# A fused attention and feed-forward kernel: the output projection in split float32r, and the last head group's projection moved into the next row

## The chip, the core and the metric

The kernel runs on one core of a Trainium2 chip. The metric is the device time of one execution in microseconds (us).

## The reference

For each of 8 rows of 512 tokens by 256 channels: layer norm without weights, then the sum of the input, an attention branch and a feed-forward branch, both fed from the normalised input.

```python
q, k = rope(xn @ Wq), rope(xn @ Wk)        # 32 query heads, 8 key heads, 64 each
v = xn @ Wv                                # 4 query heads share a key head
scores = where((j <= i) & (i - j < 128), q k^T / 8, -inf)
attn_out = (softmax(scores) @ v) @ Wo      # Wo: 2048 x 256
h = fwht(xn * SU_ug) / 64
h = silu(h @ Wgate.T * s_gate) * (h @ Wup.T * s_up)          # 1024 wide
ffn_out = (fwht(h * SU_dp) / 64) @ Wdown.T * s_down
out = x + attn_out + ffn_out
```

## The kernel before, in words

All in float32. The Hadamard transforms are folded into the weights in a prologue. Products with Wq, Wk, Wv and the gate and up weights are made from float32r operands: every operand is held as a high part (a copy rounded to float32r) and a low part (the difference), and `three` (L701) accumulates high x high, high x low and low x high. Scores, transposes, the product with V, the down projection and the output projection use plain float32; each such matmul shows as two records in the trace (a transpose as one).

After the prologue there are 8 rows (`b`). A row is:
- The feed-forward part: for j of 0 to 7 a gate and an up product (`hidden`), ScalarE's silu, VectorE's multiply, and `down(j)`. Query rope products of head groups 1 to 3 lie between them. At its end VectorE adds the result to `acc`.
- The attention part: 32 steps (8 key heads `g` by 4 blocks `i` of 128 tokens), done in 35 slots, n = 0 to LAST_SLOT. TensorE's slot n (loop at L879) issues `scores(n)`, `transposes(n-2)`, the slot's fillers, and `values_mixed(n-3)` (the product O with V). A step with i = 0 sees one block of keys, all others see two; so S of a slot with n mod 4 = 0 and O of one with n mod 4 = 3 are half as large.

`fillers(b, n)` (L81) is the hand-written order of the remaining TensorE work: V products, rope products by the table ROPE_SLOTS (L72), transposes of the next row's x (slot 25), and output projections ("wo"). An output projection `project_out(g, part)` (L854) multiplies two blocks of 128 tokens of head group g by two 128-row tiles of Wo: 4 matmuls of 256 columns, 16 such calls a row. VectorE's `wo_add` (L634) adds the result to `acc`. Before the change, the calls lie in slots 6, 7, 10, 11, ..., 30, 31, 34, and the last one after slot 34. The rope fillers are in slots 3, 4, 8, 9, 12, 13, 16, 17, 20, 21, 28, 29, and the next row's first query products in 32 and 33.

The chain of one step n across engines:
- VectorE `fold(n)` (L645): masks within S (L650) and takes the negative maximum (L652).
- ScalarE `exps(n)` (L475), which needs the maximum. `scores(n+2)` waits for it.
- VectorE `normalise(n)` (L655, in slot n+1): reciprocal and multiply.
- TensorE transposes into TR (slot n+2); ScalarE copies (L485); GpSimd masks into p_cur and p_prev (L396, L400).
- TensorE O (L849, slot n+3). It waits for the masks and, since O is one PSUM bank, for the copy of the O before it.
- ScalarE `o_copy(n)` (L487) copies O to `o_t`, as its last work of the slot; `project_out` waits for these copies by `o_copied`.

VectorE's order in a slot is fold(n), normalise(n-1), then the adds and rope multiplies of the slot's fillers. Projections, rope products, V, gate and up all take turns in the two banks of PROJ; `USES` (L99) is the list of the turns, and a user of a bank waits until the turn two before it has been read.

SP's queue issues the DMAs: for every head group, copies of rotated q and k into stacked tiles; at a row's end the output DMA, which waits for all of the row's `wo_add` (L338), and behind it the next row's stacks and the load of x. GpSimd's first work in a row is the rotation of q group 0, then it waits for the output DMA (L408) and copies x into `acc`, then come rotations 1 to 3.

In the prologue VectorE makes low parts of the weights, the rope multiplies of the first heads, and at last eight scalings of the down weights into `wd_sb` (L622). TensorE waits for them (L780) and for the DMA of Wo (L781) before row 0.

## Time and profile before

| | us |
|---|---|
| median of 3 runs | 1518.5 (1518.24 to 1518.95) |
| profiled execution | 1521.65 |
| its span, first to last instruction | 1519.8 |
| TensorE matmul busy | 1464.1 |
| VectorE busy | 1002.0 |
| ScalarE busy | 729.1 |
| GpSimd busy | 593.9 |
| mean granted TensorE clock | 0.993 |

The span is one profiled execution; the other 1.85 us of it lie around the first and last instruction. Matmuls are pipelined and their ends are modelled: the distance between starts is the pace, the duration is not. L-numbers are lines of the kernel before. In a timeline the columns are start, duration, engine, line, operation, output<-input, count, and in brackets the idle time before it with what ended it.

### The profile page before, as it was taken

The page shows a single profiled execution, that of the slowest core. Times are in us where ns is not written, and L with a number is a line of the kernel's source. Part 1 is how long each engine was busy: PE and PEld are TensorE (multiplying, and loading weights), DVE is VectorE, ACT ScalarE, POOL GpSimd, SP SyncE. Part 2 cuts the span into 40 slices and gives each one's busy share as a digit, 9 for nine tenths or more (in the row PEclk, how much of TensorE's full clock was granted, in tenths as well). Part 3 has the DMA queues.
Part 4 walks back from the last instruction along what each step waited for, and adds up shares of the span by engine and source line. Part 5 has one row for each costly group of instructions (what it writes and reads, how often), then busy time and mean ns, then how long its engine had stood idle before and what let it go on. Part 6 is the DMA issues. An engine that isn't in the chain of part 4 may idle for free. (4 is left out here: it accounts for less than half of the span.)

```text
span 1519.8 us, 25035 instructions
## 1 busy us (share of the span) xinstructions
PE 1464.1 (96%) x8424; PEld 1023.8 (67%) x8424; DVE 1002.0 (66%) x1702; ACT 729.1 (48%) x2738; POOL 593.9 (39%) x629
## 2 busy tenths in 40 slices
PE   5599999999999999999999999999999999999998
PEld 3476667766677666766668666676667766677665
DVE  5537884488835887358863788537884488835785
ACT  1226562365614656146642566326562365614655
POOL 3214543155422554125542354314543155421553
PEclk9799999999999999999999999999999999999999
DMA  7101211022020120202202111101212022020120
GB/s 285 35 21 42 51 35 53 18 56 50 22 70 20 44 51 13 69 22 56 50 19 52 43 43 43 47 23 43 55 31 57 16 58 46 22 56 21 43 54 25
DMA packets 51087, 70.67 MB, mean 46 GB/s; under 512 B 13072, under 2 KB 24848, under 8 KB 50448
## 3 DMA queue, kind: packets, MB, share of 16 engines
q1 hardware_dynamic: 49968, 68.34, 18.0%
q8 instruction: 69, 1.13, 0.3%
q10 hardware_dynamic: 992, 0.73, 0.2%
q14 instruction: 58, 0.48, 0.1%
HBM read 14.49 MB, written 4.19 MB: 12 GB/s over the span
## 5 line engine op out<-in xcount | busy, mean ns | idle before, releaser
L475 ACT ACTIVATE e_sb<-S,negmax 128x128 f32<-128x128 f32 x1024 | 361.9, 368 | 93.3 <-DVE negmax L652 93.3
L396 POOL TENSOR_SCALAR_AFFINE_SELECT p_cur<-pt_sb 128x512 f32<-128x512 f32 x256 | 185.1, 723 | 541.6 <-ACT pt_sb L485 493.0
L485 ACT ACTIVATE pt_sb<-TR 128x512 f32<-128x512 f32 x256 | 153.2, 598 | 235.8 <-PE TR L832 207.2
L823 PE MATMUL S<-k_stack,q_stack 64*128 64x256 f32 (+1 forms) x2048 | 264.5, 377 | 0.0
L861 PE MATMUL PROJ<-wo_sb,o_t 128*128 128x256 f32 x1024 | 244.2, 381 | 5.6 <-ACT o_t L490 4.6
L823 PEld LDWEIGHTS S<-k_stack,q_stack 64*128 64x128 f32 x2048 | 166.4, 187 | 106.8 <-issue 80.3
L661 DVE TENSOR_TENSOR e_sb<-e_sb,rinv 128x512 f32<-128x512 f32 x256 | 223.3, 872 | 8.7
L650 DVE COPY_PREDICATED S<-later_key,S 128x512 f32<-128x512 int8 x192 | 133.4, 695 | 132.0 <-PE S L823 132.0
L475 ACT ACTIVATION_READ_ACCUMULATOR e_sb<-S,negmax 128x1 f32 x1024 | 211.6, 207 | 0.0
L861 PEld LDWEIGHTS PROJ<-wo_sb,o_t 128*128 128x128 f32 x1024 | 184.7, 190 | 33.2 <-issue 12.6
L368 POOL TENSOR_TENSOR qy<-prod 128x512 f32<-128x512 f32 x64 | 81.6, 1275 | 291.1 <-DVE prod L573 265.9
L572 DVE TENSOR_TENSOR prod<-PROJ,cos_sb 128x512 f32<-128x512 f32 x160 | 109.4, 684 | 129.2 <-PE PROJ L705 129.2
L400 POOL TENSOR_SCALAR_AFFINE_SELECT p_prev<-pt_sb 128x512 f32<-128x512 f32 x192 | 191.8, 999 | 0.0
L652 DVE TENSOR_REDUCE negmax<-S 128x4 f32<-128x512 f32 x256 | 176.9, 691 | 8.8
L470 ACT ACTIVATE pt_sb<-PROJ 128x512 f32<-128x512 f32 x64 | 38.3, 598 | 298.8 <-PE PROJ L705 298.8
L849 PE MATMUL O<-p_cur,v_sb 128*64 128x256 f32 x1024 | 167.6, 405 | 7.2 <-POOL p_cur L396 5.4
L832 PE MATMUL TR<-ident,e_sb 128*128 128x128 f32 x1024 | 167.7, 286 | 4.8 <-DVE e_sb L661 3.1
L832 PEld LDWEIGHTS TR<-ident,e_sb 128*128 128x128 f32 x1024 | 107.2, 140 | 79.5 <-issue 57.9
L703 PE MATMUL PROJ<-xt_hi,wq_hi 128*128 128x512 f32 x256 | 116.1, 453 | 15.7 <-DVE wq_lo L530 14.5
L490 ACT ACTIVATE o_t<-O 128x256 f32<-128x256 f32 x256 | 100.1, 391 | 50.0 <-PE O L849 49.9
L632 DVE TENSOR_TENSOR p_cur<-PROJ,pt_sb 128x512 f32<-128x512 f32 x64 | 44.3, 691 | 117.4 <-PE PROJ L705 117.4
L803 PE MATMUL S<-wd_sb,p_cur 128*128 128x256 f32 x512 | 119.6, 379 | 0.0
(79 smaller groups left out, 2011.8 us busy)
## 6 DMA issues: line engine op xcount, KB each, us to landing
q_stack<-qy SPq DMA_DIRECT2D x512, 64.0 KB, 2.0
k_stack<-ky SPq DMA_DIRECT2D x256, 64.0 KB, 2.0
x_in<-x SPq DMA_DIRECT2D x8, 512.0 KB, 4.0
out<-acc SPq DMA_DIRECT2D x8, 512.0 KB, 3.1
gu_stage<-w_gate_up SPq DMA_DIRECT2D x2, 1024.0 KB, 6.5
wq_stage<-wq SPq DMA_DIRECT2D x2, 1024.0 KB, 10.1
wo_sb<-wo SPq DMA_DIRECT2D x1, 2048.0 KB, 11.0
down_stage<-w_down SPq DMA_DIRECT2D x1, 1024.0 KB, 8.5
```

The source lines that it names most:

```text
L396: nc.gpsimd.affine_select(out=p_cur[:, n % 2, :, :], in_=pt_sb[:, :, :], compare_op=ALU.is_ge, fill=0.0, base=0, pattern=[[0, REP], [1, P] ...
L400: nc.gpsimd.affine_select(out=p_prev[:, n % 2, :, :], in_=pt_sb[:, :, :], compare_op=ALU.is_gt, fill=0.0, base=0, pattern=[[0, REP], [-1, P]],
L475: last = nc.scalar.activation(e_sb[:, n % 2, r, :], s_heads(n, 1)[:, r, :], ACT.Exp, bias=negmax[:, n % 2, r:r + 1], accum_out=rowsum[:, n ...
L485: nc.scalar.activation(pt_sb[:, :, :], TR[:, :, :], ACT.Copy).then_inc(t_copied, 1)
L650: nc.vector.copy_predicated(own, later_key[:, :, :], earlier).then_inc(s_folded, 1)
L652: nc.vector.tensor_reduce(negmax[:, n % 2, :], own, axis=AX.X, op=ALU.max, negate=True).then_inc(max_done, 1)
L661: nc.vector.tensor_tensor(e, e, r, ALU.mult).then_inc(norm_done, 1)
L803: last = nc.tensor.matmul(S4[:, t, 0:C], h_sb[j % 2][:, t * P:(t + 1) * P], wd_sb[:, j, :], start=j == 0, stop=j == FT - 1)
L823: last = nc.tensor.matmul(dst, q_stack[rows, g % 2, slot, i * P:(i + 1) * P], k_stack[rows, g % 2, k0:k1], start=True, stop=True)
L832: last = nc.tensor.transpose(TR[:, r, :], e_sb[:, n % 2, r, :], ident[:, :])
L849: last = nc.tensor.matmul(O[odd * D:(odd + 1) * D, 0:2 * P].rearrange("p (m q) -> p m q", m=2), v_sb[:, i - earlier, g * D:(g + 1) * D], p ...
L861: last = nc.tensor.matmul(dst[:, t * C:(t + 1) * C], o_t[:, m, tok:tok + P], wo_sb[:, 2 * g + m, :], start=m == 0, stop=m == 1)
```

## The change

What it does:
- Wo and the attention output are held as high and low parts in float32r, and `project_out` uses `three`: 12 matmuls of 256 columns for 4.
- VectorE makes the low part of O: `o_low(n-4)` in slot n, directly behind `fold(n)`, from slot 4 on, counted by a new semaphore `o_split`. `values_mixed` and `project_out` wait for `o_split` instead of `o_copied`.
- The slots are shifted by one: projections in slots 7, 8, 11, 12, ..., 31, 32; rope parts in 9 and 10, 13 and 14, and so on; the next row's first query products in 33 and 34. Slots 5, 6 and 26 have no filler, as slots 5 and 24 had none.
- The last head group's two projections and their adds are done in the next row's feed-forward part, behind the first and second gate and up products; those of the last row at the end. So the row's output DMA waits for them there.
- In the prologue ScalarE makes the high part of Wo and VectorE the low part (4096 columns each), VectorE's ahead of the `wd_sb` scalings. TensorE waits for it before row 0. Staging tiles are laid out differently.

```diff
-    ROPE_SLOTS = {("q", 4, 0): (3, 4), ("k", 1, 0): (8, 9), ("q", 5, 0): (12, 13),
-                  ("q", 6, 0): (16, 17), ("q", 7, 0): (20, 21), ("k", 0, NEXT): (28, 29)}
+    ROPE_SLOTS = {("q", 4, 0): (3, 4), ("k", 1, 0): (9, 10), ("q", 5, 0): (13, 14),
+                  ("q", 6, 0): (17, 18), ("q", 7, 0): (21, 22), ("k", 0, NEXT): (29, 30)}
...
-        if n in (STEPS, STEPS + 1) and b + 1 < BATCH:
-            found.append(("q", b + 1, 0, n - STEPS))
-        if n >= TT + 2 and n % TT >= 2:
+        if n in (STEPS + 1, STEPS + 2) and b + 1 < BATCH:
+            found.append(("q", b + 1, 0, n - STEPS - 1))
+        if n >= TT + 3 and (n + 1) % TT < 2:
-            found.append(("wo", b, n // TT - 1, n % TT - 2))
+            found.append(("wo", b, (n + 1) // TT - 2, (n + 1) % TT))
...
+                if b and not n:
+                    USES.append(("wo", b - 1, NKV - 1, j))
...
# scalar, prologue
+            act.wait_ge(wo_in, 16)
+            nc.scalar.activation(wo_p[0][:, :, :], wo_stage[:, :, :], ACT.Copy).then_inc(w_hi, 1)
# scalar, o_copy
-                    nc.scalar.activation(o_t[:, :, i * P:(i + 1) * P],
+                    nc.scalar.activation(o_p[0][:, :, i * P:(i + 1) * P],
# vector
+            def o_low(row, n):
+                i = n % TT
+                dve.wait_ge(o_copied, row * STEPS + n + 1)
+                low(o_p[1][:, :, i * P:(i + 1) * P], O[:, 0:2 * P].rearrange("p (m q) -> p m q", m=2),
+                    o_p[0][:, :, i * P:(i + 1) * P]).then_inc(o_split, 1)
...
             products(0, "q", 0, 1)
+            dve.wait_ge(w_hi, CT + 2)
+            low(wo_p[1][:, :, :], wo_stage[:, :, :], wo_p[0][:, :, :]).then_inc(w_lo, 1)
...
-                hidden(0)
-                hidden(1)
+                for j in HIDDEN_AFTER[0]:
+                    hidden(j)
+                    if b:
+                        if not j:
+                            o_low(b - 1, STEPS - 1)
+                        wo_add(b - 1, NKV - 1, j)
...
                     if n < STEPS:
                         fold(n)
+                    if 4 <= n:
+                        o_low(b, n - 4)
                     if 1 <= n <= STEPS:
                         normalise(n - 1)
...
-                wo_add(NKV - 1, 1)
+            o_low(BATCH - 1, STEPS - 1)
+            for part in range(2):
+                wo_add(BATCH - 1, NKV - 1, part)
# tensor
+            def project_out(row, g, part):
+                dst = bank("wo", row, g, part)
+                pe.wait_ge(o_split, row * STEPS + TT * g + 2 * part + 2)
+                for t in range(2):
+                    for m in range(2):
+                        tok = (2 * part + t) * P
+                        last = three(dst[:, t * C:(t + 1) * C], [a[:, m, tok:tok + P] for a in o_p],
+                                     [a[:, 2 * g + m, :] for a in wo_p], m == 0, m == 1)
+                last.then_inc(proj_ready, 1)
...
-            pe.wait_ge(wo_in, 16)
+            pe.wait_ge(w_lo, CT + 2)
...
                     if n >= 1:
-                        pe.wait_ge(o_copied, b * STEPS + n)
+                        pe.wait_ge(o_split, b * STEPS + n)
...
                             hidden(name, j)
+                        if b and not n:
+                            project_out(b - 1, NKV - 1, j)
                         if j:
                             down(j - 1)
...
-                project_out(NKV - 1, 1)
+            for part in range(2):
+                project_out(BATCH - 1, NKV - 1, part)
```

## Rows read from the trace of the kernel before

**Rows 1.** The page's first part: busy us, share of the span, instructions.
```profile
PE 1464.1 (96%) x8424; PEld 1023.8 (67%) x8424; DVE 1002.0 (66%) x1702; ACT 729.1 (48%) x2738; POOL 593.9 (39%) x629
```

**Rows 2.** Stretches: length, busy of PE, PEld, DVE, ACT, POOL, granted clock; one feed-forward part.
```profile
429.20:476.40 47.20, 47.05 (x204) 37.90 (x202) 17.03 (x31) 9.04 (x13) 8.58 (x7) 1.00 0.21 56
```

**Rows 3.** Timelines of TensorE and of VectorE, slots 12 and 13 of row 3.
```profile
702.74 0.71 PE L823 MATMUL S<-k_stack,q_stack 64*128 64x128 f32 x8
...
705.37 0.65 PE L849 MATMUL O<-p_cur,v_sb 128*64 128x256 f32 x4
...
706.39 1.13 PE L823 MATMUL S<-k_stack,q_stack 64*128 64x256 f32 x8
...
709.44 0.65 PE L849 MATMUL O<-p_cur,v_sb 128*64 128x256 f32 x4
...
710.45 0.49 PE L823 MATMUL S<-k_stack,q_stack 64*128 64x256 f32 x2
...
703.62 0.75 DVE L650 COPY_PREDICATED_SCALAR S<-later_key,masked 128x512 f32 x1 [0.56 <-PE S L823]
...
707.68 0.70 DVE L650 COPY_PREDICATED S<-later_key,S 128x512 f32<-128x512 int8 x1 [0.48 <-PE S L823]
708.41 0.69 DVE L652 TENSOR_REDUCE negmax<-S 128x4 f32<-128x512 f32 x1
709.02 0.17 DVE L657 RECIPROCAL rinv<-rowsum 128x4 f32<-128x4 f32 x1
```

**Rows 4.** Timeline of TensorE: an output projection, and two float32r matmuls of a rope product.
```profile
700.34 1.89 PE L861 MATMUL PROJ<-wo_sb,o_t 128*128 128x256 f32 x8
...
704.12 0.41 PE L704 MATMUL PROJ<-xt_lo,wq_hi 128*128 128x512 f32 x1
...
705.06 0.39 PE L705 MATMUL PROJ<-xt_hi,wq_lo 128*128 128x512 f32 x1
```

**Rows 5.** Groups by line and form, VectorE adds from PSUM: busy us, mean ns.
```profile
L642 DVE TENSOR_TENSOR acc<-PROJ,acc 128x512 f32<-128x512 f32 x128 | 87.1, 680 | 40.6 <-PE PROJ L861 40.6
...
L676 DVE TENSOR_TENSOR acc<-S,acc 128x1024 f32<-128x1024 f32 x8 | 9.8, 1225 | 21.5 <-PE S L803 21.5
```

**Rows 6.** Timelines: a rotation; slots 8, 24, 28 of row 1; 24 and 31 of row 7.
```profile
312.87 1.26 POOL L368 TENSOR_TENSOR qy<-prod 128x512 f32<-128x512 f32 x1 [2.65 <-PE O L849]
...
322.41 0.71 PE L823 MATMUL S<-k_stack,q_stack 64*128 64x128 f32 x8
...
386.73 0.71 PE L823 MATMUL S<-k_stack,q_stack 64*128 64x128 f32 x8
...
389.92 1.68 DVE L556 TENSOR_SCALAR prod<-x_in,moments,rstd 128x256 f32<-128x256 f32 x4
...
401.73 0.72 PE L823 MATMUL S<-k_stack,q_stack 64*128 64x128 f32 x8
...
1479.40 0.71 PE L823 MATMUL S<-k_stack,q_stack 64*128 64x128 f32 x8
...
1502.80 1.14 PE L823 MATMUL S<-k_stack,q_stack 64*128 64x256 f32 x8
```

**Rows 7.** Timeline from slot 31 of row 1 into the feed-forward part of row 2.
```profile
413.83 1.14 PE L823 MATMUL S<-k_stack,q_stack 64*128 64x256 f32 x8
...
419.51 0.37 ACT L490 ACTIVATE o_t<-O 128x256 f32<-128x256 f32 x1
...
420.02 0.65 PE L849 MATMUL O<-p_cur,v_sb 128*64 128x256 f32 x4 [0.15 <-ACT o_t L490]
...
427.62 1.97 PE L861 MATMUL PROJ<-wo_sb,o_t 128*128 128x256 f32 x8 [0.57 <-ACT o_t L490]
429.24 0.59 PE L703 MATMUL PROJ<-xt_hi,wgu_hi 128*128 128x512 f32 x1
```

**Rows 8.** The prologue: timeline of VectorE, and a stretch (0.57 is the clock).
```profile
59.67 3.43 DVE L622 SCALAR_TENSOR_TENSOR wd_sb<-S,su_mid_sb,o_t 128x256 f32<-128x256 f32 x8
...
40.00:60.00 20.00, 7.06 (x16) 5.02 (x17) 14.29 (x14) 6.77 (x6) 4.65 (x3) 0.57 0.06 14
```

More of the change, by code:

```diff
@@ L109, in attention_and_ffn_block @@
             USES += fillers(b, n)
-        USES.append(("wo", b, NKV - 1, 1))
+    USES += [("wo", BATCH - 1, NKV - 1, part) for part in range(2)]
     TURN = {what: u for u, what in enumerate(USES)}
@@ L134, in sem @@
             return ctx.enter_context(nc.semaphore(name))
-        wq_p = [sb(f"wq_{s}", [P, CT, NH * D], f32r) for s in ("hi", "lo")]
-        wk_p = [sb(f"wk_{s}", [P, CT, NKV * D], f32r) for s in ("hi", "lo")]
-        wv_p = [sb(f"wv_{s}", [P, CT, NKV * D], f32r) for s in ("hi", "lo")]
+        with ExitStack() as prologue:
+            wq_stage = prologue.enter_context(nc.sbuf_tensor("wq_stage", [P, CT, NH * D], fp32))
+            wo_stage = prologue.enter_context(nc.sbuf_tensor("wo_stage", [P, NH * D // P, C], fp32))
+            kv_stage = prologue.enter_context(nc.sbuf_tensor("kv_stage", [P, 2, CT, NKV * D], fp32))
+        wq_lo = sb("wq_lo", [P, CT, NH * D], f32r)
+        wo_lo = sb("wo_lo", [P, NH * D // P, C], f32r)
+        wk_lo = sb("wk_lo", [P, CT, NKV * D], f32r)
+        wv_lo = sb("wv_lo", [P, CT, NKV * D], f32r)
+        wq_p = [sb("wq_hi", [P, CT, NH * D], f32r), wq_lo]
+        wo_p = [sb("wo_hi", [P, NH * D // P, C], f32r), wo_lo]
+        wk_p = [sb("wk_hi", [P, CT, NKV * D], f32r), wk_lo]
+        wv_p = [sb("wv_hi", [P, CT, NKV * D], f32r), wv_lo]
         wgu_p = [sb(f"wgu_{s}", [P, CT, 2 * F], f32r) for s in ("hi", "lo")]
         wd_sb = sb("wd_sb", [P, FT, C])
-        wo_sb = sb("wo_sb", [P, NH * D // P, C])
         cos_sb = sb("cos_sb", [P, T])
@@ L164, in attention_and_ffn_block @@
         with ExitStack() as prologue:
-            wq_stage = prologue.enter_context(nc.sbuf_tensor("wq_stage", [P, CT, NH * D], fp32))
             gu_stage = prologue.enter_context(nc.sbuf_tensor("gu_stage", [P, CT, 2 * F], fp32))
@@ L171, in attention_and_ffn_block @@
         k_stack = sb("k_stack", [P, 2, T])
-        staging_rest = sb("staging_rest", [P, 5120])
+        o_lo = sb("o_lo", [P, REP // 2, T], f32r)
         ky = sb("ky", [P, 2, T])
@@ L181, in attention_and_ffn_block @@
         p_prev = sb("p_prev", [P, 2, REP, P])
-        o_t = sb("o_t", [P, REP // 2, T])
+        scale_d_b = sb("scale_d_b", [P, C])
+        had = sb("had", [P, 2, P])
+        o_p = [sb("o_hi", [P, REP // 2, T], f32r), o_lo]
         xn = prod[:, 0:2, :].rearrange("p a (t c) -> p (a t) c", c=C)
@@ L574, in products, with wo_add @@
                                         ).then_inc(prod_done, 1)
+            def o_low(row, n):
[3 more added lines that the diff above has]
+                    o_p[0][:, :, i * P:(i + 1) * P]).then_inc(o_split, 1)
+            def wo_add(row, g, part):
+                bank, filled = place("wo", row, g, part)
+                k = 2 * g + part
+                dve.wait_ge(proj_ready, filled)
+                if k >= 2:
+                    dve.wait_ge(wo_added, (row + 1) * 2 * NKV + k - 1)
+                a = acc[:, 2 * part:2 * part + 2, :]
+                nc.vector.tensor_tensor(a, PROJ[:, bank, :].rearrange("p (t c) -> p t c", t=2), a, ALU.add
+                                        ).then_inc(wo_added, 1)
             row_stats(0)
@@ L632, in hidden @@
                     nc.vector.tensor_tensor(h_sb[j % 2], PROJ[:, bank, :], silu_sb, ALU.mult).then_inc(h_done, 1)
-                def wo_add(g, part):
-                    bank, filled = place("wo", b, g, part)
-                    k = 2 * g + part
-                    dve.wait_ge(proj_ready, filled)
-                    if k >= 2:
-                        dve.wait_ge(wo_added, (b + 1) * 2 * NKV + k - 1)
-                    a = acc[:, 2 * part:2 * part + 2, :]
-                    nc.vector.tensor_tensor(a, PROJ[:, bank, :].rearrange("p (t c) -> p t c", t=2), a, ALU.add
-                                            ).then_inc(wo_added, 1)
                 def fold(n):
@@ L691, in _ @@
                         if kind == "wo":
-                            wo_add(m, part)
+                            wo_add(row, m, part)
                         elif kind == "x":
@@ L852, in values_mixed @@
                     last.then_inc(pv_done, 1)
-                def project_out(g, part):
-                    dst = bank("wo", b, g, part)
-                    pe.wait_ge(o_copied, b * STEPS + TT * g + 2 * part + 2)
-                    for t in range(2):
-                        for m in range(2):
-                            tok = (2 * part + t) * P
-                            last = nc.tensor.matmul(dst[:, t * C:(t + 1) * C], o_t[:, m, tok:tok + P],
-                                                    wo_sb[:, 2 * g + m, :], start=m == 0, stop=m == 1)
-                    last.then_inc(proj_ready, 1)
                 for n in range(4):
@@ L885, in _ @@
                         if kind == "wo":
-                            project_out(m, part)
+                            project_out(row, m, part)
                         elif kind == "x":
```

28 lines of the change are left out of this document (11 added, 17 removed).

## The prediction

> **What bounds the kernel now.** I read the page first: TensorE is busy 96% of the span, VectorE 66%, ScalarE and GpSimd under half [rows 1]. That says TensorE, but a matmul's recorded end is modelled, so the pace has to be read from starts. The stretch table of a feed-forward part shows TensorE without gaps [rows 2]. Then I read slots of the attention part, from one scores group to the next [rows 3]. A slot is S, transposes, a filler, O. The slots at 702.74 and 706.39 last 3.65 and 4.06 us, and no row of TensorE in them has an idle stretch ahead of it; the longer one has scores of two key blocks. Slots come in periods of four, two with a rope filler and two with an output projection: slots 8 to 23 of that row last 386.73-322.41 = 64.32 us [rows 6], 16.08 a period, and it is TensorE's own work.
>
> The second thing to see in [rows 3] is how close VectorE runs behind. The fold of step n starts 0.88 us after S where S has one block (703.62) and 1.29 us where it has two (707.68). Ahead of them it idled 0.56 and 0.48 us only. From the fold to the end of the reduce is 1.42 us (707.68 to 709.10), while O starts 2.63 and 3.05 us after S.
>
> **Part 1, the projection itself.** One call was 8 records of 256 columns in 1.89 us, the last lasting 0.38: (1.89-0.38)/7 = 0.216 us each, 1.73 in all [rows 4]. It becomes 12 float32r matmuls of 256 columns. The trace has float32r at 512 columns only: four steps from 704.12 to 705.06, 0.235 us each [rows 4]. From below: one pass of 256 columns is half of 0.216, 0.108 us. From above: the cost belongs to the instruction and not to its columns, 0.235. The 512-column row exceeds 0.216 by 0.019; if that excess is fixed, 256 columns take 0.127. I take this, since two fp32 passes of 256 and one float32r pass of 512 agree so nearly that the rate per column is the same. A call is then 1.52 us, 0.21 less; 128 calls save 27 us of TensorE. The ends give 1.30 and 2.82 us.
>
> The weight loads matter here: twelve loads of 128 columns against eight, and half as many columns streamed behind each. The trace shows loads of full 128-row weights keeping up with fp32 matmuls 0.216 apart [rows 4]. The Trainium skill's "TensorE: Matmul & The Clock Gate", in Part 3 on packing small matmuls, says a weight load overlaps a running matmul only where the row group differs. By that rule load and matmul would add up and the projection would lose by the change; in this trace the row group is the same and the pace is still that of the streaming alone, so the rule does not hold for it as stated.
>
> **Part 2, o_low and the wait on it.** VectorE gets one more instruction per step, 256 in all: O (256 columns, PSUM) minus the high part. A PSUM add of 512 columns is 0.68 us and one of 1024 is 1.225 [rows 5]; the slope gives 0.41 us at 256. Behind another instruction it occupies about 0.34, as neighbours overlap by 0.08. Its place is behind the fold: fold, o_low(n-4), normalise(n-1). And O of step n-3 now waits for that o_low instead of for ScalarE's copy. Behind the waiting O on TensorE are the next scores, thus the next fold and everything else.
>
> So a slot has a floor that it did not have. Where S has two blocks: fold at 1.29, reduce 0.73 later, o_low 0.61 after that (708.41 to 709.02), its end 0.41 on: 3.04 us after S. From the release to the start of O is 0.14 (copy end 419.88, O 420.02) [rows 7]. O starts at 3.18, and the next S 1.01 later (709.44 to 710.45): a floor of 4.19, or 3.76 where O has one block. With one block of scores (a fold of 0.75 where the other is 0.70) it is 0.88+0.79+0.61+0.41+0.14 = 2.83, and 3.84 in all. The new order puts the projections in slots with n mod 4 of 3 and 0, the rope parts in 1 and 2. TensorE alone would need 4.06 in a rope slot and 4.06+1.52-6 x 0.235-0.43 = 3.74 in one with a projection and one block of S or O. The floor is at or above each: 3.84+4.19+4.19+3.76 = 15.98 against 16.08 now. Of the 0.43 that the two projections save, 0.33 is given to the wait. Four periods (slots 8 to 23) in eight rows: 32 x -0.10 = **-3.2 us**. VectorE's load is no bound there: o_low takes 0.34 of the 0.5 us it idled.
>
> **Part 3, slots without a filler.** These were short, since O had nothing to wait for. In slots 4 to 7 the mask waits for a rotation that starts at 312.87, held by a DMA, so slot 6 was already stalled. Following it through with the floor, O of slot 5 starts 1.7 us later, O of slot 6 0.6 later, and the scores of slot 8 come at 322.4 as before [rows 6]: **0**. But one projection fewer lies in the stalled stretch, and is paid elsewhere (below).
> Slots 24 to 27 were 401.73-386.73 = 15.0 us [rows 6]. Now: 3.84; then slot 25, whose fold comes 0.6 late behind four normalisations (1.68 in all) and the projection's add, 4.79; slot 26 without a filler 4.19; slot 27 3.76. Sum 16.58, 1.58 more, **+11.0** in seven rows. Slots 28 to 30: 3.84+4.19+4.19 = 12.22 against 12.12, **+0.7**.
> The last row has no work of a next row, so slots 25, 26, 29 and 30 are empty: slots 24 to 30 were 1502.80-1479.40 = 23.40 [rows 6], now 15.98+12.22 = 28.20: **+4.8**.
>
> **Part 4, the row's end.** From the scores of slot 31 (413.83) to the feed-forward part (429.24) is 15.4 us; it holds three projections, and a stall of 0.57 ahead of the last [rows 7], which goes. Now slot 31 takes 3.76. In slot 32 o_low(28) waits for a copy that lies behind a table load and ends at 419.88, 6.04 after slot 31's scores; O starts at 6.65 instead of 5.9, and the next transposes at 7.67. The rest is 5.6: 13.3. Two projections follow in the feed-forward part, where nothing hides them (TensorE had no gap [rows 2]): 3.04. Together 16.3, +0.93 a row, **+6.5** in seven. The output DMA now starts some 9 us later, and behind it in SP's queue stand the next row's stack copies and its x load, in GpSimd's the copy into acc and rotation 1. The rotation needs products that come 15 us into the feed-forward part, the scores need the stacks 47 us in: cost 0. Without that slack it would be the delay itself.
> In the last row o_copy, o_low and O alternate for three steps with nothing beside them, and two projections follow: **+1.1**.
>
> **Part 5, the prologue.** wo needs a high part (ScalarE, idle then: 0) and a low part of 4096 columns, which stands on VectorE ahead of the eight scalings of wd at 59.67, and TensorE waits for both [rows 8]. At the slope of [rows 5] it is 4.5 us: from below. It reads two SBUF tiles while GpSimd rotates; if it were held up as long as those run, 2.5 us more: from above. I take 4.5: the nearest row, the scalings at 59.67, ran beside that rotation at 0.43 each, not held up. The Trainium skill's "SBUF — State Buffer", section on the two sides, says whichever of the two starts first has the shared ports for its whole instruction; by it 4.5 if VectorE wins the race and 2.5 more if GpSimd does; no row shows which. TensorE then idles 5.5 us and not 1. From 40 to 60 us, with TensorE busy 7 of 20, the mean granted clock was 0.57 [rows 8], so mostly the lower of the two levels (1.2 and 2.4 GHz): it had fallen while TensorE idled and rose only after it had resumed. An estimate: half rate for the first 4 us of row 0 costs 2 (0 to 3). **+6.5**.
>
> **Sum**: -3.2+11.0+0.7+4.8+6.5+1.1+6.5 = +27.4 us. The profiled execution took 1521.65 (span 1519.8), so 1549.05; the median of the runs is 1518.5, 3.15 less, so 1545.9: forecast **1546**.
>
> **Rivals.**
> B, it gets faster: O never waits for o_low, TensorE's own work is the sum. For it: 96% busy. The point that decides is whether o_low has ended by 2.9 to 3.1 us after S. Then -27, a row's last stall gone (8 x -0.6 = -5), one projection out of the stalled slots (8 x 1.5 = +12), prologue +6.5: -13.5, **1505**. Against it: [rows 3] put the fold's end at 2.7 alone. 0.13.
> C, a float32r matmul of 256 columns costs as much as one of 512 (0.235), since it is bound by something other than its columns, the weight load say. A call is 2.82 us. In slots with a projection TensorE then exceeds the floor by 1.2: 14 x 8 x 1.2 = 134, and 16 in the feed-forward parts cost 1.3 more, 21: **1700**. The rule in the skill's TensorE page is this rival's mechanism, with load and matmul in series. 0.07.
> D, the floor holds only where there is no filler, because o_low ends some 0.1 us sooner than I put it: the periods get 15.65, so -0.33 x 32, and slots 28 to 30 -0.25 x 8: **1533**. 0.13.
> E, as forecast, and TensorE's longer idling in slots 4 to 7 lowers its clock in each row as it did in the prologue [rows 8]. 3.4 us at half rate is 1.7 a row, 14 in all: **1560**. 0.07.
> My forecast: 0.60.
>
> **Range.** The pace of 0.108 takes 3 off, one of 0.14 adds 13; the latencies (0.05 per slot, 230 slots) are worth 12 either way; the prologue -2 to +4. With D and E inside: 1524 to 1572. B and C are left out, 0.20. A measurement of this kernel can tell about 0.2%, 3 us. Faster: B, and little of D: 0.14. Same: 0.03. Slower: 0.83.
>
> **What the changed profile would show.** Starts of the projection's matmuls 0.127 us apart; o_low at 0.41; ahead of O an idle stretch put down to VectorE's o_lo, near 0.1 us in filled slots and 1.5 in empty ones; slots of 4.19; the first gate matmul at about 68 us. I am wrong if O starts as soon as its filler ends (B), if the projection's starts are over 0.2 apart (C), or if slots 25 and 26 together stay under 8 us.

## The result, and the profile after

The changed kernel takes **1547.8 us** (median of 4 runs, 1546.6 to 1547.8) where the kernel before takes 1518.4 (4 runs, 1517.1 to 1519.0): ratio 1.0193, 95% interval 1.0175 to 1.0211. The forecast was 1546. The profiled execution has a span of 1546.1 us, 26.3 more than before; the mean granted clock is 0.992.

The page's first part, then three groups by line and form (busy us, mean ns, idle time before with its releasers):

```profile
PE 1429.3 (92%) x8936; PEld 1041.7 (67%) x8936; DVE 1095.0 (71%) x1959; ACT 744.3 (48%) x2739; POOL 544.0 (35%) x629
```

```profile
L885 PE MATMUL O<-p_cur,v_sb 128*64 128x256 f32 x1024 | 167.2, 398 | 70.3 <-DVE o_lo L538 42.1 <-POOL p_cur L406 14.7
...
L730 PE MATMUL PROJ<-wo_hi,o_lo 128*128 128x256 f32 x512 | 143.6, 281 | 0.0
...
L538 DVE TENSOR_TENSOR o_lo<-O,o_hi 128x256 fp32r<-128x256 f32 x256 | 106.5, 416 | 16.2 <-ACT o_hi L501 15.6
```

Against [rows 1], TensorE is busy 35 us less and the span is 26 us longer. The wait is new: 42.1 us of TensorE's idle time end with o_lo, all of it ahead of O. The transposes wait 2.7 us for VectorE's normalisation. The idle time is not the loss. 23.5 of the 42.1 us lie in slots 5 and 6. Slot 6 was stalled before the change too (it took 5.28 us in row 1), and slots 0 to 7 are no longer than they were (the table below). On the other side, part of the time that the projections save went into slots whose projection now ends earlier and whose O does not.

TensorE and VectorE in slots 8 and 9 of row 3 (one block of scores with a projection, then two blocks with a rope part; [rows 3] has slots 12 and 13):

```profile
697.62 0.74 DVE L667 COPY_PREDICATED_SCALAR S<-later_key,masked 128x512 f32 x1
697.66 0.36 PE L728 MATMUL PROJ<-wo_hi,o_hi 128*128 128x256 f32 x1
...
698.09 0.28 PE L728 MATMUL PROJ<-wo_hi,o_hi 128*128 128x256 f32 x1
...
698.80 0.28 PE L728 MATMUL PROJ<-wo_hi,o_hi 128*128 128x256 f32 x1
...
699.00 0.41 DVE L538 TENSOR_TENSOR o_lo<-O,o_hi 128x256 fp32r<-128x256 f32 x1
699.03 0.28 PE L730 MATMUL PROJ<-wo_hi,o_lo 128*128 128x256 f32 x1
...
699.56 0.65 PE L885 MATMUL O<-p_cur,v_sb 128*64 128x256 f32 x4 [0.25 <-DVE o_lo L538]
...
700.58 1.14 PE L859 MATMUL S<-k_stack,q_stack 64*128 64x256 f32 x8
701.87 0.70 DVE L667 COPY_PREDICATED S<-later_key,S 128x512 f32<-128x512 int8 x1 [0.82 <-PE S L859]
702.60 0.69 DVE L669 TENSOR_REDUCE negmax<-S 128x4 f32<-128x512 f32 x1
703.21 0.41 DVE L538 TENSOR_TENSOR o_lo<-O,o_hi 128x256 fp32r<-128x256 f32 x1
...
703.77 0.65 PE L885 MATMUL O<-p_cur,v_sb 128*64 128x256 f32 x4
...
704.79 1.14 PE L859 MATMUL S<-k_stack,q_stack 64*128 64x256 f32 x8
```

From 698.09 to 698.80 are six steps from one matmul of 256 columns to the next, 0.118 us each. The last projection matmul starts at 699.03, o_lo ends at 699.41, O starts at 699.56: 0.15 later. In the next slot the same chain, fold 1.29 after S, reduce, o_lo, O 0.15 after that, makes 704.79-700.58 = 4.21 us.

With no filler the wait is bare. TensorE in slots 5 and 6 of row 1, and these two slots as stretches (length, busy of PE, PEld, DVE, ACT, POOL, clock, DMA):

```profile
318.09 0.65 PE L885 MATMUL O<-p_cur,v_sb 128*64 128x256 f32 x4 [1.47 <-DVE o_lo L538]
...
322.30 0.65 PE L885 MATMUL O<-p_cur,v_sb 128*64 128x256 f32 x4 [1.47 <-DVE o_lo L538]
```

```profile
314.90:319.11 4.21, 2.74 (x23) 1.68 (x21) 4.05 (x8) 2.49 (x11) 1.23 (x1) 1.00 0.27 62
319.11:323.31 4.20, 2.73 (x22) 1.68 (x20) 3.08 (x6) 1.65 (x8) 3.36 (x5) 1.00 0.00 0
```

The prologue, where [rows 8] stood, and the first stretch of row 0:

```profile
58.03 4.42 DVE L538 TENSOR_TENSOR wo_lo<-wo_stage,wo_hi 128x4096 fp32r<-128x4096 f32 x1
58.19 5.38 POOL L378 TENSOR_TENSOR qy<-prod 128x512 f32<-128x512 f32 x1 [14.88 <-DVE prod L584]
62.36 3.22 DVE L650 SCALAR_TENSOR_TENSOR wd_sb<-S,su_mid_sb,scale_d_b 128x256 f32<-128x256 f32 x8
...
65.68 0.76 PE L728 MATMUL PROJ<-xt_hi,wgu_hi 128*128 128x512 f32 x1 [5.46 <-DVE wd_sb L650]
```

```profile
65.60:77.40 11.80, 11.72 (x43) 9.54 (x44) 2.18 (x4) 1.20 (x2) 0.17 (x1) 0.82 0.34 90
```

The span up to the start of the last matmul, cut at the starts of S and of the first gate product of each row. Times are in us, summed over the rows named; where a mean is given, its difference is the sum over the seven rows.

| stretch | before | after | difference |
|---|---|---|---|
| up to the first gate matmul | 63.20 | 65.68 | +2.5 |
| feed-forward of row 0 | 47.14 | 48.99 | +1.9 |
| feed-forward, rows 1 to 7, mean | 47.24 | 49.95 | +19.0 |
| slots 0 to 7, 8 rows | 226.1 | 223.1 | -3.0 |
| slots 8 to 23, 8 rows | 514.6 | 514.9 | +0.3 |
| slots 24 to 27, rows 0 to 6 | 105.0 | 116.9 | +11.9 |
| slots 28 to 30, rows 0 to 6 | 84.9 | 86.6 | +1.7 |
| slot 31 to the feed-forward part, rows 0 to 6 | 107.8 | 93.0 | -14.8 |
| last row, slots 24 to 30 | 23.40 | 28.42 | +5.0 |
| last row, slot 31 to the last matmul | 12.50 | 14.38 | +1.9 |

They sum to +26.4, the difference of the spans but for rounding. In slots 8 to 23 nothing is left of what the projection saves: a call takes 1.73-1.42 = 0.31 us less of TensorE, the 64 calls there 20 us, and the stretch is as long as before.

### The profile page after: what moved, and what is told of

Same layout as the page of the kernel before. It is cut to its first block, busy times and chain, and to the rows that moved or that the text cites. A ratio compares the mean times of both kernels' runs of the same rounds, so it can differ in the third digit from the quotient of the medians.

```text
span 1546.1 us, 26317 instructions
## 1 busy us (share of the span) xinstructions
PE 1429.3 (92%) x8936; PEld 1041.7 (67%) x8936; DVE 1095.0 (71%) x1959; ACT 744.3 (48%) x2739; POOL 544.0 (35%) x629
## 3 DMA queue, kind: packets, MB, share of 16 engines
HBM read 14.49 MB, written 4.19 MB: 12 GB/s over the span
## 4 chain that ended last, share of the span: by engine, by line
PE 64%; DVE 21%; ACT 5%; issue 5%; POOL 4%; DMA 0%; POOLq 0%; ACTq 0%; DVEq 0%
PE S L859 13%; PE O L885 13%; PE PROJ L728 9%; PE PROJ L730 8%; PE PROJ L729 8%; PE S L839 7%; PE TR L868 5%; DVE S L667 5%; DVE negmax L669 5%; POOL p_cur L406 4%; ACT pt_sb L496 3%; DVE o_lo L538 2%; DVE prod L583 2%; DVE e_sb L678 2%; DVE prod L584 2%
## 5 line engine op out<-in xcount | busy, mean ns | idle before, releaser
L678 DVE TENSOR_TENSOR e_sb<-e_sb,rinv 128x512 f32<-128x512 f32 x256 | 229.1, 895 | 8.7
L885 PE MATMUL O<-p_cur,v_sb 128*64 128x256 f32 x1024 | 167.2, 398 | 70.3 <-DVE o_lo L538 42.1
L378 POOL TENSOR_TENSOR qy<-prod 128x512 f32<-128x512 f32 x64 | 85.8, 1341 | 301.6 <-DVE prod L584 274.2
L728 PE MATMUL PROJ<-wo_hi,o_hi 128*128 128x256 f32 x512 | 152.7, 298 | 0.0
L885 PEld LDWEIGHTS O<-p_cur,v_sb 128*64 128x64 f32 x1024 | 57.4, 135 | 140.5 <-POOL p_cur L406 70.9
L730 PE MATMUL PROJ<-wo_hi,o_lo 128*128 128x256 f32 x512 | 143.6, 281 | 0.0
L729 PE MATMUL PROJ<-wo_lo,o_hi 128*128 128x256 f32 x512 | 143.2, 280 | 0.0
L410 POOL TENSOR_SCALAR_AFFINE_SELECT p_prev<-pt_sb 128x512 f32<-128x512 f32 x192 | 134.1, 698 | 0.0
```

Of the source, the lines that this page charges most:

```text
L678: nc.vector.tensor_tensor(e, e, r, ALU.mult).then_inc(norm_done, 1)
L728: nc.tensor.matmul(dst, lhs[0], rhs[0], start=first, stop=False)
L729: nc.tensor.matmul(dst, lhs[0], rhs[1], start=False, stop=False)
L730: return nc.tensor.matmul(dst, lhs[1], rhs[0], start=False, stop=last)
L885: last = nc.tensor.matmul(O[odd * D:(odd + 1) * D, 0:2 * P].rearrange("p (m q) -> p m q", m=2), v_sb[:, i - earlier, g * D:(g + 1) * D], p ...
```

## The experiments

The theory is the prediction's: O waits for o_low behind the fold, which sets a floor for each slot. Rivals after the result: VectorE is simply too full for 256 more instructions; the new order itself is what costs; float32r at 256 columns gains too little. Ratios are against the kernel before, run beside each of them: median 1518.1 for experiments 3, 10 and 11, and 1518.7 or 1518.8 for the others.

**1. o_low ahead of the fold.** The same instructions, in another order.

```diff
+                    if 4 <= n:
+                        o_low(b, n - 4)
                     if n < STEPS:
                         fold(n)
-                    if 4 <= n:
-                        o_low(b, n - 4)
```

> The changed kernel with one edit: VectorE does o_low(n-4) ahead of fold(n) and not behind it. The work of every engine is the same. Theory A (O waits for an o_low that stands behind the fold, which sets a floor of 4.2, 3.85 or 3.77 us per slot): o_low is done by about 1.4 us after the scores, before O wants to start even in a slot without filler, so slots fall to TensorE's own work. Periods of four: 3.67+4.06+4.06+3.67 = 15.5 instead of 16.07, four of them in 8 rows -18; slots 24 to 27 about 15.2 instead of 16.67 in seven rows, -10; slots 28 to 30 -0.5 each row, -4; the last row's slots 24 to 30 about 21.8 instead of 28.4, -6; slots 5 to 7 stay bound by the rotation. About 1508 us, faster than both kernels. Rival (VectorE's added load itself holds TensorE up): the load is unchanged, so 1540 or more.

Measured: **1513.1** us, ratio 0.9956 (0.9940 to 0.9972): 34.7 us come back, and this version is a little faster than the kernel before. TensorE and VectorE in slot 9 of row 3:

```profile
689.68 1.14 PE L859 MATMUL S<-k_stack,q_stack 64*128 64x256 f32 x8
690.32 0.42 DVE L538 TENSOR_TENSOR o_lo<-O,o_hi 128x256 fp32r<-128x256 f32 x1 [0.42 <-ACT o_hi L501]
...
690.98 0.70 DVE L667 COPY_PREDICATED S<-later_key,S 128x512 f32<-128x512 int8 x1 [0.24 <-PE S L859]
...
692.75 0.65 PE L885 MATMUL O<-p_cur,v_sb 128*64 128x256 f32 x4
...
693.76 1.14 PE L859 MATMUL S<-k_stack,q_stack 64*128 64x256 f32 x8
```

o_lo stands in time in which VectorE waited for S anyway, its copy having ended: the fold still starts 1.30 us after S, as in [rows 3]. O starts with no idle time ahead of it, and the slot is 4.08. Slots 8 to 23 take 61.8 us a row instead of 64.4. The expectation said 1508, though its own four terms add up to -38 and so to 1510. Those stretches gave -36 between the traces (-20.8, -9.8, -1.6 in seven rows, -4.2), and slots 0 to 7 gave +1.1 instead of nothing. The clock is in that +1.1: its falls cost these slots some 11 us in this execution. Slots 5 and 6 of two rows (columns as above; the windows of the first row are cut at 862.00, and its slot 6 ends at 861.41):

```profile
853.90:856.80 2.90, 2.75 (x22) 1.68 (x20) 2.87 (x6) 1.48 (x6) 0.18 (x1) 1.00 0.40 90
856.80:862.00 5.20, 3.59 (x25) 2.01 (x25) 4.09 (x8) 2.95 (x14) 4.36 (x5) 0.93 0.01 3
862.00:866.60 4.60, 4.60 (x30) 3.34 (x26) 3.08 (x6) 3.12 (x16) 1.49 (x3) 0.71 0.19 43
...
1034.40:1037.30 2.90, 2.75 (x22) 1.68 (x20) 2.87 (x6) 1.48 (x6) 0.12 (x1) 1.00 0.40 90
1037.30:1042.00 4.70, 3.04 (x24) 1.57 (x22) 4.15 (x8) 2.39 (x11) 4.00 (x4) 1.00 0.02 3
```

In the first row the granted clock falls behind the stall of slot 6, in the second it does not. Slots 0 to 7 take 28.2 to 28.7 us in the rows where it falls and 26.6 where it does not. It falls in six rows of this execution. The runs scatter from 1506 to 1516, the shorter ones with the higher mean clock (0.985 to 0.991).

**2. o_low cut loose from O.** It subtracts the high part from itself, so that the low part of the attention output is zero, and O waits for the copy alone.

```diff
-                low(o_p[1][:, :, i * P:(i + 1) * P], O[:, 0:2 * P].rearrange("p (m q) -> p m q", m=2),
+                low(o_p[1][:, :, i * P:(i + 1) * P], o_p[0][:, :, i * P:(i + 1) * P].bitcast(fp32),
...
-                        pe.wait_ge(o_split, b * STEPS + n)
+                        pe.wait_ge(o_copied, b * STEPS + n)
```

> The changed kernel with o_low in its place behind the fold, 256 of them, but reading only the high part in SBUF (so the low part of the attention output is zero: that part of the product is left out), and O waiting for ScalarE's copy alone, as before the change. Theory A: the load without the wait costs nearly nothing, 1500 to 1510 us. Rival (VectorE's load): still 1540 or more. Both its inputs are in SBUF, so it may be held up at times where GpSimd works, which could add some us.

Measured: **1533.2** us, ratio 1.0099 (1.0079 to 1.0120), a miss. The wait of O is gone, and another stands in its place, together with a longer o_lo. Two groups of this kernel:

```profile
L868 PE MATMUL TR<-ident,e_sb 128*128 128x128 f32 x1024 | 167.7, 286 | 46.0 <-DVE e_sb L678 44.0 <-ACT pt_sb L496 1.6
...
L538 DVE TENSOR_TENSOR o_lo<-o_hi 128x256 fp32r<-128x256 f32 x256 | 147.7, 577 | 11.6 <-ACT o_hi L501 11.0
```

The transposes now wait 44 us for the normalisation, and o_lo takes 577 ns where it took 416. VectorE and GpSimd of row 3:

```profile
700.91 0.63 POOL L406 TENSOR_SCALAR_AFFINE_SELECT p_cur<-pt_sb 128x512 f32<-128x512 f32 x1 [2.65 <-ACT pt_sb L496]
701.03 0.79 DVE L538 TENSOR_TENSOR o_lo<-o_hi 128x256 fp32r<-128x256 f32 x1
...
704.97 0.63 POOL L406 TENSOR_SCALAR_AFFINE_SELECT p_cur<-pt_sb 128x512 f32<-128x512 f32 x1 [2.66 <-ACT pt_sb L496]
705.29 0.59 DVE L538 TENSOR_TENSOR o_lo<-o_hi 128x256 fp32r<-128x256 f32 x1
```

Both times o_lo ends 0.28 us after GpSimd's mask (701.54 and 701.82, 705.60 and 705.88), whenever it began. The experiment had a side effect of its own: by reading SBUF in place of PSUM, o_lo became an instruction that waits for GpSimd.

**3. The same with one SBUF input.** o_low multiplies the high part by zero; the low part of the attention output is zero.

```diff
+                nc.vector.tensor_scalar(o_p[1][:, :, i * P:(i + 1) * P],
+                    o_p[0][:, :, i * P:(i + 1) * P].bitcast(fp32), 0.0, None, ALU.mult).then_inc(o_split, 1)
...
+                        pe.wait_ge(o_copied, b * STEPS + n)
```

> As the kernel with o_low cut loose from O (1533.2), but o_low reads one SBUF tile instead of two: a multiplication of the high part by zero (the low part of the attention output is zero in both). It must still end before nobody's O; only normalise stands behind it. Theory P: the 1533 came from two SBUF inputs that share something with GpSimd (o_low took 577 ns on average, 1432 at most). Then o_low now takes under 350 ns each time, normalise goes back to about 895 ns, slots 12, 16 and 20 to 3.66, and the total is about 1506 (range 1502 to 1512). Theory L: VectorE has simply no room for one more instruction ahead of normalise, whatever it reads. Then the transposes still wait for normalise and it stays above 1522.

Measured: **1525.6** us, ratio 1.0049 (1.0032 to 1.0066). The time is on the side of theory L (over 1522), and the transposes wait 34.6 us for the normalisation; but the condition for telling P from L, an o_lo under 0.35 us each time, was not met, since the mean is 0.526. The 39 o_lo with no GpSimd instruction beside them take 0.28 to 0.30 us; the longest are 1.42:

```profile
901.78 1.27 POOL L380 TENSOR_TENSOR qy<-prod 128x512 f32<-128x512 f32 x1
901.79 1.42 DVE L590 TENSOR_SCALAR o_lo<-o_hi 128x256 fp32r<-128x256 f32 x1
...
903.33 0.92 DVE L678 TENSOR_TENSOR e_sb<-e_sb,rinv 128x512 f32<-128x512 f32 x1
...
904.30 0.66 PE L868 MATMUL TR<-ident,e_sb 128*128 128x128 f32 x4 [0.80 <-DVE e_sb L678]
```

So the contention does not need two SBUF inputs, and theory P named its cause too narrowly. Held-up o_lo and late normalisation lie on one path, and these two kernels do not say how much VectorE's plain load would cost alone. They cannot be read as the price of a kernel whose O never waits; experiments 1 and 5 can.

**4. The projection back in fp32.** 4 fp32 matmuls of the high parts; the low parts are made and waited for, and not used.

```diff
-                        last = three(dst[:, t * C:(t + 1) * C], [a[:, m, tok:tok + P] for a in o_p],
-                                     [a[:, 2 * g + m, :] for a in wo_p], m == 0, m == 1)
+                        last = nc.tensor.matmul(dst[:, t * C:(t + 1) * C], o_p[0][:, m, tok:tok + P].bitcast(fp32),
+                                                wo_p[0][:, 2 * g + m, :].bitcast(fp32), start=m == 0, stop=m == 1)
```

> The changed kernel with the output projection as 4 plain float32 matmuls of the high parts (the low parts are left out of the product), everything else, o_low and its wait too, in place. Theory A: in slots the projection takes 0.31 us more (1.73 against 12 x 0.118), but 0.1 to 0.2 of it lies under the floor: TensorE's own slot is 3.96 against floors of 3.77 and 3.85, so 14 x 0.15 a row, and 2 x 0.33 in the feed-forward part: 8 x 2.8 = +22, about 1570 us. Rival (TensorE is the bound and every us of it counts): 128 x 0.31 = +40, 1588 us.

Measured: **1565.0** us, ratio 1.0309 (1.0294 to 1.0324). It is 5 us under theory A's number and 23 under the rival's. Float32r is worth 17 us in the changed kernel. At 0.31 us a call, 128 calls are 40 us; the rest is hidden under the floor (slots 8 to 23 grow by 8.7 us for 20 us of TensorE).

**5. No low part of O.** The projection multiplies the high part twice, so that the term with the low part of O is not the reference's; there is no o_low, and O and the projection wait for the copy. All matmuls stay.

```diff
-                    if 4 <= n:
-                        o_low(b, n - 4)
...
-                        last = three(dst[:, t * C:(t + 1) * C], [a[:, m, tok:tok + P] for a in o_p],
+                        last = three(dst[:, t * C:(t + 1) * C], [o_p[0][:, m, tok:tok + P]] * 2,
...
-                        pe.wait_ge(o_split, b * STEPS + n)
+                        pe.wait_ge(o_copied, b * STEPS + n)
```

> The changed kernel without o_low: the third matmul of each product uses the high part of the attention output again (12 matmuls and 12 loads as before; the low part is left out), O and the projection wait for ScalarE's copy. Theory A: as low_first and a little lower at the row's end, where O no longer waits for the copy behind the table load plus o_low (-0.4 a row): about 1503 us. Against the changed kernel it gives the price of o_low and its wait together, about 45 us. Rival B of the prediction, which put the kernel at 1505 without the wait, is tested by it too.

Measured: **1501.3** us, ratio 0.9891 (0.9876 to 0.9906), as expected. One group of it:

```profile
L880 PE MATMUL O<-p_cur,v_sb 128*64 128x256 f32 x1024 | 167.4, 405 | 19.8 <-POOL p_cur L406 15.9 <-ACT o_hi L501 3.9
```

o_low with its wait costs 46 us. Experiment 1 keeps the instruction and gives back 35 of them, so the instruction costs some 12 where it stands ahead of the fold, and its place behind the fold the rest. Rival B's sum of 1505 for a kernel whose O never waits is near this 1501; only its condition is not met by the change.

**6. The order alone.** Both edits above, with the fp32 projection and with no low part of Wo either: the new slots and the moved projections of the last head group are all that is left of the change (besides the names of tiles).

```diff
-                    if 4 <= n:
-                        o_low(b, n - 4)
...
+                        last = nc.tensor.matmul(dst[:, t * C:(t + 1) * C], o_p[0][:, m, tok:tok + P].bitcast(fp32),
...
-            low(wo_p[1][:, :, :], wo_stage[:, :, :], wo_p[0][:, :, :]).then_inc(w_lo, 1)
```

> The order alone: slots shifted by one and the last group's projections in the next row's feed-forward part, but the projection as 4 plain float32 matmuls (of the operands' high parts), no o_low, no low part of Wo, and O waiting for ScalarE's copy. Theory A (the order costs: one projection of 1.73 us leaves slots 6 and 7, where TensorE waits for the rotation anyway, +14 in 8 rows; the stall of 0.6 at the row's end goes, -5; with longer idling in slot 5 and 6 the clock falls once a row, 1.7 each as in the run without o_low, +12 or less): 1535 us. Rival (the order is what helps, since it takes a stall away and hides the projections in the feed-forward part): 1510 to 1515 us.

Measured: **1535.7** us, ratio 1.0113 (1.0098 to 1.0128). The new order costs 17 us by itself (14 between the two traces, since the one of the kernel before lies 3 above its median): the feed-forward parts take 3.36 longer, a row's end 2.37 less (seven rows: +7), and slots 0 to 7, with a projection fewer in them and the clock falling, +8 in all. With 4, 5 and the changed kernel it makes a square: fp32 without low parts 1535.7, float32r without 1501.3, fp32 with 1565.0, float32r with 1547.8. The square has a flaw: 1535.7 alone has no low part of Wo, and with it goes 7.0 us up to the end of row 0's feed-forward part (108.8 against 115.8 in experiment 5). So float32r is worth 34 us with that price in it and about 41 without, where O does not wait, which is what 128 calls at 0.31 give, and 17 where it does. In all rows of experiment 6 the clock falls once around slot 6, and slots 0 to 7 take 28.8 to 29.8 us.

**7. The old order, with o_low ahead of the fold.** Old slots and old row end, float32r, low parts; o_low as in experiment 1.

```diff
-    ROPE_SLOTS = {("q", 4, 0): (3, 4), ("k", 1, 0): (9, 10), ("q", 5, 0): (13, 14),
-                  ("q", 6, 0): (17, 18), ("q", 7, 0): (21, 22), ("k", 0, NEXT): (29, 30)}
+    ROPE_SLOTS = {("q", 4, 0): (3, 4), ("k", 1, 0): (8, 9), ("q", 5, 0): (12, 13),
+                  ("q", 6, 0): (16, 17), ("q", 7, 0): (20, 21), ("k", 0, NEXT): (28, 29)}
...
-        if n >= TT + 3 and (n + 1) % TT < 2:
+        if n >= TT + 2 and n % TT >= 2:
-            found.append(("wo", b, (n + 1) // TT - 2, (n + 1) % TT))
+            found.append(("wo", b, n // TT - 1, n % TT - 2))
```

> float32r projection and o_low, o_low(n-4) ahead of fold(n) as in low_first (1513 us), but with the slots and the row's end of the kernel before. Theory A: projections return to slots 6 and 7, where TensorE waits (8 x 1.4 = -11), the clock no longer falls in each row (up to -12), the row's end has its stall back and o_low in it (+0.6 to +1 a row, +7): about 1497 us. Rival (the shift was needed for o_low, the second projection of a group now waits for an o_low of the same slot): over 1513 us.

Measured: **1515.2** us, ratio 0.9977 (0.9968 to 0.9987), a miss by 18. Slots 0 to 7 gained only 2.2 us in all on experiment 1: the clock does not fall here, which was to bring up to 12, but the projection that is back in them was not free, as the expectation had it. And a wait that it priced at the row's end only stands in other slots too: the second projection of a group waits for an o_low of its own slot, 17.8 us in 25 places (7.2 at the rows' ends, 4.9 in slot 27, 4.2 in slot 7). Against the kernel before, the row's end grows from 15.40 to 15.96 and slots 24 to 27 from 14.99 to 15.77, the prologue and row 0 cost 5.4 more, and slots 8 to 23 gain 2.0 a row where the projections save 2.5.

**8. The old order, with o_low behind the fold.**

> As order_back, but o_low behind the fold, as the change has it: float32r and o_low without the change of order. Theory A: the second projection of each group needs an o_low that ends 3.04 us after the slot's scores, and starts at 3.18 instead of 1.5; with 1.42 for itself and 0.68 up to the next scores that slot lasts 5.3 instead of 3.8, seven times a row: +84, less about 11 for a projection back in the stalled slots, so about 1600 us. It shows what the shift by one slot was good for. Rival (VectorE's load or TensorE's work is the bound, the places don't matter): 1550 us or less.

Its edit is that of 7 without the move of o_low. Measured: **1621.1** us, ratio 1.0676 (1.0660 to 1.0692), some 20 above the expectation. VectorE and TensorE, a slot with n mod 4 = 3:

```profile
719.74 1.13 PE L851 MATMUL S<-k_stack,q_stack 64*128 64x256 f32 x8
...
722.38 0.42 DVE L535 TENSOR_TENSOR o_lo<-O,o_hi 128x256 fp32r<-128x256 f32 x1
...
722.94 0.35 PE L720 MATMUL PROJ<-wo_hi,o_hi 128*128 128x256 f32 x1 [1.47 <-DVE o_lo L535]
...
725.07 0.71 PE L851 MATMUL S<-k_stack,q_stack 64*128 64x128 f32 x8
```

In the old slot the projection itself needs the O of the slot before, waits 1.47 us for o_lo, and the slot takes 5.33. That is what the shift by one slot is for: with o_low behind the fold the new order saves 73 us. With o_low ahead of it, 1515.2 and 1513.1 are not told apart.

**9. Two more waits out of the old order.** As 7; the low part of Wo is made ahead of the first query products of the prologue, and ScalarE copies O of step 28 before it loads the table for silu.

```diff
+            dve.wait_ge(w_hi, CT + 2)
+            low(wo_p[1][:, :, :], wo_stage[:, :, :], wo_p[0][:, :, :]).then_inc(w_lo, 1)
             products(0, "q", 0, 0)
             products(0, "q", 0, 1)
-            dve.wait_ge(w_hi, CT + 2)
-            low(wo_p[1][:, :, :], wo_stage[:, :, :], wo_p[0][:, :, :]).then_inc(w_lo, 1)
...
-                    if n == STEPS - 1 and b + 1 < BATCH:
-                        load_table(ACT.Silu)
...
                     if n >= 3:
                         o_copy(n - 3)
+                    if n == STEPS - 1 and b + 1 < BATCH:
+                        load_table(ACT.Silu)
```

> As order_back with two edits more: the low part of Wo is made ahead of the first query heads' rope multiplies, where VectorE waits for TensorE (about -3 us in the prologue and less idling of TensorE before row 0), and ScalarE copies O of step 28 ahead of the table load in slot 31 and not behind it, which takes the stall in slot 32 away (-0.6 a row, -4). About 1490 us, the fastest so far.

Measured: **1504.0** us, ratio 0.9904 (0.9890 to 0.9919). As a number it misses by 14, nearly all of it taken over from experiment 7, which was expected at 1497. The two edits were to bring 7 and brought 11.2: the first gate matmul comes at 63.40 instead of 66.61, a row's end takes 15.03 instead of 15.96, which is 3.2 and 6.5 us.

**10. The same, with the last group's projections in the next row.** 9, and of the change's order only this part.

```diff
-        if n >= TT + 2 and n % TT >= 2:
+        if TT + 2 <= n < NKV * TT and n % TT >= 2:
```

> As the best kernel so far (old slots, o_low ahead of the fold, low part of Wo early, copy of O ahead of the table load; 1504.0), but the last group's two projections go into the next row's feed-forward part. The row's end loses two projections (2.8) and the wait ahead of them, the feed-forward part gains 2.7 (49.95 against 47.25). Theory M: the move is worth only the row's last stalls, about 0.4 a row, so 1501 (range 1498 to 1504). Rival R: the output DMA, about 9 us later, comes too late for the next row's stacks or rotations; slots 0 to 7 (27.8 us before) grow by 1 us or more in a row, so over 1508.

Measured: **1503.5** us, ratio 0.9905 (0.9888 to 0.9922), the same as 9. A row's end falls by 3.09, the feed-forward part grows by 2.89, and slots 8 to 30 stay within 0.1 a row. Slots 0 to 7 are within 0.2 in rows 2 to 7, all of which follow a later output DMA; row 0, which has none ahead of it, takes 1.1 more and row 1 0.7, with the clock at full speed. So the later output DMA, which rival R was about, costs nothing that the rows show.

**11. The new order with experiment 1 and the two edits of 9.**

> The new order kept whole, with o_low ahead of the fold (1513.1), the low part of Wo made before the first rope multiplies, and the copy of O of step 28 ahead of the table load. From the old order these last two brought 3.2 in the prologue and about 0.9 at a row's end. Expected 1513.1 - 3.2 - 7 x 0.5 = 1506 (range 1502 to 1511). It still has the clock falling to half for 3.4 us in slots 5 and 6 of most rows; if that were gone, 12 us more would go, 1494.

Measured: **1502.3** us, ratio 0.9900 (0.9885 to 0.9915), at the low end of its range (1502 to 1511). Of the versions that do the whole computation, this, 9 and 10 are the fastest, 1% below the kernel before; these runs do not tell the three apart. Experiments 1 and 7 are below it too, by 0.4% and 0.2%. The page's first part and the group of O:

```profile
PE 1422.5 (95%) x8936; PEld 1026.7 (68%) x8936; DVE 1082.6 (72%) x1959; ACT 727.5 (48%) x2739; POOL 557.3 (37%) x629
```

```profile
L885 PE MATMUL O<-p_cur,v_sb 128*64 128x256 f32 x1024 | 167.0, 404 | 27.5 <-DVE o_lo L538 14.2 <-POOL p_cur L406 12.1
```

VectorE is nearly as busy as in the changed kernel (1082.6 and 1095.0 us); the span is 46 us shorter. So the rival that VectorE is simply too full is out. Of the 14.2 us that O still waits for o_lo, 11.3 lie in slot 26, which has no filler. Giving O two halves of its PSUM bank in turn, so that it need not wait for o_low, wasn't tried.

## Why the prediction was right

It put the loss in the wait of O for o_low. Experiment 1 shows that o_low's place makes it: the same instructions in another order give 34.7 us back. That edit also takes o_low out from between fold and normalisation, so by itself it does not say which wait it was; the trace of the changed kernel does, with 42.1 us of waits for o_lo ahead of O, 2.7 for the normalisation ahead of the transposes, and slots at the floors that were worked out. Experiments 2 and 3 show that the second wait stands right behind the first: once O waited for the copy alone, the transposes waited 44 and 35 us. By the forecast's own steps:

- **Part 1, the pace.** 0.127 us was forecast between 0.108 and 0.235; 0.118 was measured. It lies near half of 0.216 plus a small excess, and a call is about 1.42 us, 12 steps, where 1.52 was forecast. That is why the feed-forward part grew by 2.71 and not 3.04. The Trainium skill's "TensorE: Matmul & The Clock Gate", Part 3, lets a weight load overlap a running matmul only where the row group differs. The trace does not agree: full 128-row loads, one row group, and starts 0.118 us apart. Rival C, which needed more than 0.2, falls with it.
- **Part 2, the floor.** o_low at 0.41 us was 0.416. The floors of 3.84, 4.19, 4.19 and 3.76 were 3.85, 4.21, 4.21 and 3.77. These 0.01 to 0.02, one slot in 16 of 3.98 where 3.84 was forecast, and 0.6 in two slots of row 1 (4.08 and 4.56) turn the forecast -3.2 into +0.3. Rival D had these slots at TensorE's own time. They are so in experiment 1 (4.08 and 3.65), with o_low in another place, and not in the changed kernel.
- **Part 3, slots without a filler.** Slots 24 to 27: +1.7 for +1.58 each. The last row: +5.0 for +4.8. Slots 0 to 7 were forecast at 0 and gave -3.0, of which 2.3 lie in row 0, where before the change the clock fell behind slot 6 and after it did not. So rival E's falls did not come, and one that was there went away. In the changed kernel the idle time of slots 5 and 6 is cut in two pieces of 1.47 us; whether that is the reason was not tested.
- **Part 4, the row's end.** 13.3 was forecast, 13.27 measured. With the feed-forward part it makes +4.1 in all for +6.5, since the pace was 0.118. The late output DMA cost nothing, as argued; experiment 10 shows it. The last row's tail was +1.9 for +1.1; O waits twice for o_lo there, 0.45 and 1.02 us.
- **Part 5, the prologue.** The low part of Wo was put at 4.5 and took 4.42; TensorE idled 5.46 for a forecast 5.5. The stretch grew by only 2.5, since the low part started at 58.03 where the scalings had started at 59.67: in this execution the clock rose 2.84 us earlier in the prologue (at 21.98 for 24.82, and again at 56.11 for 58.95). Whether the change has a part in that was not tried; in the experiments with the same prologue (1 to 5, 7 and 8) the first gate matmul comes at 65.4 to 66.6, 2.2 to 3.4 after the 63.20 of before. The half-rate start of row 0 cost 1.9 for 2. Of the two sides of the race that the forecast left open, VectorE started first, at 58.03 against 58.19, and GpSimd's rotation took 5.38 us for 1.27. By the rule of the Trainium skill's "SBUF — State Buffer", the section on the two sides, the one that starts first keeps the ports for its whole instruction. The trace agrees: the rotation ends at 63.57, 1.12 us after the low part.

The sum was +27.4 for a measured +26.3. The forecast took 3.15 off, since the profiled execution before was so far above its median; the one after took 1547.8, which is its median, and so the median came out 1.8 above the forecast though the sum was 1.1 too high. Its parts are right in kind, with errors of up to 3.5 us. That the sum is right to 1 us is partly luck: the terms that came out higher were 6.5 us too low together, the others 7.6 too high. What it did not say is that the wait could be had for nothing: it called VectorE's idle 0.5 us ahead of the fold no bound, and did not go on to ask why o_low does not stand in it.

## What to carry to other kernels

A new instruction on an engine that is two thirds busy is not priced by its duration but by what stands ahead of it in that engine's order when its input is ready, and by who waits for its end. Look for the idle stretch of that engine in the slot and put the instruction ahead of the wait that ends it: here that alone was worth 35 us, twice the 17 that the faster matmuls gave in the changed kernel. A faster filler gives nothing more once it ends ahead of what the next instruction waits for, and work between two waits on the critical chain should be compared with that floor before it is made shorter.

## What the runs showed of the hardware

- A float32r matmul of 256 columns with a 128 by 128 weight load takes 0.118 us in a row of them, half of the 0.235 of one of 512: the load stays hidden behind half as many columns too.
- An o_lo that read SBUF alone waited for a GpSimd instruction that ran already (in experiment 2 it ends 0.28 us after it in 167 of 175 cases): with two inputs it took 0.42 us when free and up to 1.43 (experiment 2), with one input 0.28 when free and up to 1.42, beside a rotation of 1.27 (experiment 3). In the prologue it was the other way round: a rotation of 1.27 took 5.38 beside the low part of Wo. All 256 o_lo of the changed kernel, which read PSUM and SBUF, took 0.41 to 0.43, 228 of them beside a GpSimd instruction. The Trainium skill's "SBUF — State Buffer", section on the two sides, names VectorE instructions with two SBUF inputs and those in a mode that uses two ports. The trace agrees on the first; that the one-input o_lo ran in such a mode is not shown.
- The granted clock fell to its half level (1.2 of 2.4 GHz) behind the stall of slot 6 in six rows of experiment 1 and in every row of experiment 6, and in no row of the changed kernel, where slots 5 and 6 have TensorE busy 2.74 of 4.21 and 2.73 of 4.20 us. In experiment 1 it fell in row 4 and not in row 5, with the same busy time in slot 5 (2.75 of 2.90) and a slot 6 of the same length (4.6). Each fall cost about 1.8 us. What decides it was not settled.
